# The wide layer norm's sum of squares by two transposes and a VectorE reduction, with two ScalarE steps moved

## The reference

```
x = norm(x + L0(x, adj))   # hypergraph convolution to 512 features, relu, layer norm with gamma and beta,
                           # hypergraph convolution back to 256, + x
x = norm(x + L1(x, adj))   # relu([x, adj @ x / degree] @ W.T)
x = norm(x + L2(x, adj))   # three GCN layers: adj @ (x @ W) + b, relu after the first two
x = norm(x + L3(x, adj))   # relu(adj @ x @ kernel), masked where a row of x is all zero
```

```
var = mean(h * h) - mean(h)**2;  (h - mean) * rsqrt(var + 1e-5) * gamma + beta
```

## Time and profile before

| | |
|---|---|
| time, median of 3 runs | 1382.65 us (1382.41 to 1382.7) |
| the profiled execution's own time | 1382.37 us |
| its span, first to last instruction | 1380.6 us |
| PE busy | 1365.6 us, 99% |
| VectorE (DVE) busy | 1168.3 us, 85% |
| ScalarE (ACT) busy | 1115.1 us, 81% |
| GpSimd (POOL) busy | 1032.8 us, 75% |
| DMA, share of 16 engines, main queue | 16.3% |
| mean granted clock of TensorE | 0.999 |

### The profile page before, as it was taken

How to read it: one execution, slowest core, us unless ns; L and a number is a source line. 1 busy time by engine, 2 the same in 40 slices (tenths; PEclk the granted TensorE clock), 3 DMA queues, 4 the chain that set the end, 5 groups by cost and what they waited for, 6 DMA issues and landing times.

```text
span 1380.6 us, 35393 instructions
## 1 busy us (share of the span) xinstructions
PE 1365.6 (99%) x10836; PEld 1324.6 (96%) x10836; DVE 1168.3 (85%) x4037; ACT 1115.1 (81%) x2584; POOL 1032.8 (75%) x1114
## 2 busy tenths in 40 slices
PE   8999999999999999999999999999999999999997
PEld 7999999999999999999999999999999999999996
DVE  8888888888888888888888888888888888888896
ACT  6777887888888878878878888888788788888776
POOL 5758778778788787787787787877877877878531
PEclk9999999999999999999999999999999999999999
DMA  4101211211211112111112111111121121121000
GB/s 144 36 20 24 47 44 29 47 43 29 44 35 40 44 28 47 44 28 47 43 29 47 36 35 44 28 47 44 29 47 44 29 47 43 28 45 34 2 24 32
DMA packets 45804, 54.45 MB, mean 39 GB/s; under 512 B 12208, under 2 KB 28080, under 8 KB 45616
## 3 DMA queue, kind: packets, MB, share of 16 engines
q1 hardware_dynamic: 45616, 52.19, 16.3%
HBM read 35.33 MB, written 16.83 MB: 38 GB/s over the span
## 4 chain that ended last, share of the span: by engine, by line
PE 97%; ACT 1%; issue 1%; DMA 0%; SPq 0%; DVE 0%; POOL 0%; ACTq 0%; DVEq 0%; POOLq 0%
PE psum L400 95%; PE psum L499 2%; DMA r_f<-w1T_in 0%; PE psum L443 0%; ACT x L1034 0%; SPq L305 0%; ACT tk L1203 0%; ACT h_hi L1015 0%; SPq L338 0%; ACT h_f L1039 0%; DVE n_st L1605 0%; DVE n_s L274 0%; DVE xbw_lo L1670 0%; SPq L342 0%; ACT w1T_hi L1015 0%
## 5 line engine op out<-in xcount | busy, mean ns | idle before, releaser
L1034 ACT ACTIVATE x<-n_s,n_shift,n_rstd 128x256 f32<-128x256 f32 x384 | 208.8, 593 | 4.7 <-DVE n_shift L1629 4.1
L222 POOL TENSOR_TENSOR h_lo<-h_f,h_hi 128x512 fp32r<-128x512 f32 x120 | 155.0, 1292 | 57.7 <-ACT h_hi L1015 56.8
L229 POOL TENSOR_TENSOR r_lo<-r_f,r_hi 128x512 fp32r<-128x512 f32 x123 | 157.3, 1293 | 43.5 <-ACT r_hi L1015 43.5
L2292 POOL TENSOR_TENSOR n_s<-tk,mask 128x512 f32<-128x512 f32 x60 | 62.4, 1041 | 156.2 <-DVE mask L1682 135.2
L1605 DVE BATCH_NORM_STATS2 n_st<-n_s 128x6 f32<-128x256 f32 x384 | 141.9, 412 | 2.2
L400 PE MATMUL psum<-v_hi,h_hi 128*128 128x256 f32 x512 | 137.8, 291 | 2.0 <-ACT h_hi L1015 2.0
L1039 ACT ACTIVATE h_f<-psum,columns 128x256 f32<-128x256 f32 x256 | 107.6, 472 | 35.1 <-PE psum L400 35.0
L400 PE MATMUL psum<-A_f,x 128*128 128x128 f32 x1024 | 135.3, 275 | 0.6 <-ACT x L1034 0.5
L400 PE MATMUL psum<-v_lo,h_hi 128*128 128x256 f32 x512 | 132.7, 281 | 0.0
L400 PE MATMUL psum<-gx_hi,w1T_hi 128*128 128x256 f32 x512 | 132.2, 281 | 0.0
L400 PE MATMUL psum<-gx_hi,w1T_lo 128*128 128x256 f32 x512 | 131.9, 280 | 0.0
(11 more groups left out here) (177 smaller groups left out, 5159.8 us busy)
## 6 DMA issues: line engine op xcount, KB each, us to landing
x_in<-x_in_dram SPq DMA_DIRECT2D x64, 256.0 KB, 2.8
out<-x SPq DMA_DIRECT2D x64, 256.0 KB, 2.0
at_in<-adjT SPq DMA_DIRECT2D x64, 128.0 KB, 2.3
dinv_b<-dinv_row SPq DMA_DIRECT2D x55, 128.0 KB, 4.1
dinv_row<-dinv SPq DMA_DIRECT2D x55, 1.0 KB, 3.1
x<-v_in SPq DMA_DIRECT2D x3, 256.0 KB, 5.8
n_s<-w2T_in SPq DMA_DIRECT2D x2, 256.0 KB, 3.0
r_f<-w1T_in SPq DMA_DIRECT2D x2, 256.0 KB, 5.1
```

Of the source, the lines that this page charges most:

```text
L222: return e.tensor_tensor(dst[1][:], src, f(dst[0][:]), ALU.subtract).then_inc(signal, 1)
L229: e.tensor_tensor(r_s[1][:, half], r_f[:, half], f(r_s[0][:, half]), ALU.subtract).then_inc(r_lo[h], 1)
L1034: last = act.activation(dst[:, g, :], nm.s[:, g, :], ACT.Identity, scale=nm.rstd[:, g:g + 1], bias=nm.shift[:, g:g + 1])
L2292: pool.tensor_tensor(n4.s[:], tk[:], bc(mask[:], [C, 2, D], 2), ALU.mult).then_inc(tk_masked, 1)
```

## The change

The pairs whose squares fall in the loop no longer sum over partitions by matmuls with ones. PE transposes the two halves of `sq1` into columns 384 to 511 of P's two banks, and VectorE reduces these 2 x 128 columns to the two values in column 258, ahead of the variance, in a new step that waits for P's signal and for `h_mean2`. A new semaphore, `sq_added`, stands between it and the variance. In ScalarE's loop `make_x3(n-4)` goes ahead of `root_h(n-1)`, and `copy_h1w(n-3)` ahead of `round_p(n-1)`. Fill and drain keep their order and their matmuls.

```diff
@@ in the semaphores
+        sq_added = sem("sq_added")
@@ PE
             def squares(p):
                 pe.wait_ge(sq_sum, upto(p))
+                if in_loop(p, 1):
+                    for g in range(2):
+                        last = pe.transpose(psum[:, bank("P", p) + g, 3 * C:4 * C], sq1[:, g, :], ident[:])
+                    last.then_inc(pe_did["P"], 1)
+                    return
                 for g in range(2):
                     last = mm(psum[:, bank("P", p) + g, D + 2:D + 3], sq1[:, g, :], ones[:, 0:1], True, True)
                 last.then_inc(pe_did["P"], 1)
@@ ScalarE, body(n)
                 square_mean(n - 1)
                 round_GT(n)
+                make_x3(n - 4)
                 root_h(n - 1)
-                make_x3(n - 4)
+                copy_h1w(n - 3)
                 round_p(n - 1)
-                copy_h1w(n - 3)
                 high_ax3(n - 4)
@@ VectorE
+            def add_columns(p):
+                b = bank("P", p)
+                dve.wait_ge(pe_did["P"], upto(p))
+                dve.wait_ge(hm2, upto(p))
+                if begun(p - 1):
+                    dve.wait_ge(hv, upto(p - 1))
+                dve.tensor_reduce(psum[:, b:b + 2, D + 2], psum[:, b:b + 2, 3 * C:4 * C], AX_X, ALU.add).then_inc(sq_added, 1)
+
             def wide_var(p):
                 b = bank("P", p)
+                if in_loop(p, 1):
+                    add_columns(p)
+                    dve.wait_ge(sq_added, p + 2 - FIRST)
                 h_var = psum[:, b:b + 2, D + 4]
```

## The result

The changed kernel took 1393.31 us (median of 4, 1391.87 to 1393.45) against 1382.56 us for the kernel before, run beside it (4 runs, 1382.41 to 1382.7). The ratio is 1.0071, 95% interval 1.0059 to 1.0083: slower by 0.7%. The forecast was 1393 us.

The account below looks back on a forecast made before the run. PE, busy 99%, was taken to bound the kernel. Cheaper squares give -13.2 us and 55 waits of 0.43 us for x1 add 23.6, so +10.4 on 1382.65 makes 1393.1 us; 8-in-10 range 1384 to 1402.

Parts of the forecast that it names:

- D (p_f): Lateness of p_f on VectorE after the squares' first load, against 1.70: 0.71 us, bounds 0.62 and 0.89.
- p_lo's load, wanted 5.27: PE's load of p_lo: operand ends 5.30 to 5.43, wanted at 5.27; wait of 0.1 to 0.2 us likely.
- xT to squares: PE's work from xT's first load back to the next squares, closing the period's circle: 10.57 us.
- period: One loop iteration, from squares through ScalarE, VectorE, x1 and xT back to squares: 21.22 us against 21.03.
- What PE gains: Squares on PE: two transposes, 0.22 us, replace matmuls of 0.46; 0.24 us an iteration, 13.2 us over 55.
- What the delay costs: x1 0.71 us late makes PE wait 0.43 us at xT in each of 55 iterations: 23.6 us.
- GpSimd's part: GpSimd's scaling of GT ends late, at 0.63, so GT's rounding starts at 0.68 instead of 0.60; adds 0.09.
- rival (a): Only the direct delay counts, GT in time: D 0.62, period 21.13, +5.5 us, 1388 us; chance 0.22.
- The sum: Whole kernel: -13.2 us gained on PE plus 23.6 us of waits, +10.4 us, 1393.1 us; chance 0.46.
- PE's busy share: Sign in the changed profile: PE's busy share falls below 99%.
- Rival (c): Faster: VectorE finds room or the root slips less; PE keeps up to 0.24 us an iteration, 1369.4 us; chance 0.12.
- The rule on transposes: Skill's some 275 ns per transpose on PE: two take 0.55 us, squares cost 0.09 more, 5 us over the loop.

Follow-up runs that it names:

- the version without waits: Changed kernel with GT's rounding behind the root, p_lo ahead of the addition xb on GpSimd, and node_degree ahead of make_p: 1368.06 us, ratio 0.9893.
- The pair of kernels with five equal moves: Gx ahead of Ax3, gx_hi, wide variance, gx_lo and p_lo moved earlier: 1388.75 us with transposes and reduction, 1384.18 us on the kernel before with matmuls.
- the order alone: Kernel before with only ScalarE's new order (x3 ahead of the root, h1w ahead of p's rounding), squares by matmuls: 1394.59 us, ratio 1.0084.
- the short reduction: Changed kernel with VectorE's reduction over 2 instead of 128 columns: 1393.09 us, ratio 1.0068.
- the degrees ahead of p: Changed kernel with VectorE's node_degree (two tiny operations) moved ahead of make_p: 1371.20 us, ratio 0.9912.
- GT's rounding behind the root: Changed kernel with round_GT moved behind root_h on ScalarE: 1385.63 us, ratio 1.0018.
- Gx ahead of Ax3 with transposes: Changed kernel with PE's Gx ahead of Ax3, ScalarE's old order with gx_hi ahead of ax3_hi, wide variance ahead of n4's shift: 1391.40 us, ratio 1.0057.

## Why the prediction was right

Point by point, the forecast beside the row of the kernel after:

| step | forecast | measured |
|---|---|---|
| squares on PE | 0.22 | 0.21 |
| reduction | 0.42 at 0.85 | 0.43 at 0.85 |
| mean's square | 0.53 | 0.52 |
| GT's rounding | 0.68 | 0.68 |
| x3, root | 1.00, 1.98 | 1.00, 1.99 |
| D (p_f) | 0.71 | 0.71 |
| x1 ends | 10.60 | 10.60 |
| p_lo's load, wanted 5.27 | 5.3 to 5.5 | 5.43 |
| xT's first load | 10.65 | 10.66 |
| xT to squares | 10.57 | 10.54 |
| period | 21.22 | 21.20 |

- **What PE gains** was 0.25 us (forecast 0.24), and is shown to be there to take: the version without waits is at 20.75, 0.28 under the old period. Of the other 0.03 the runs show no cause. The pair of kernels with five equal moves does not show the gain, since x1's wait takes more than all of it.
- **What the delay costs** is shown by the order alone (x1's wait without any transpose), by the short reduction (nothing), and by the degrees ahead of p, which takes x1's lateness away while the root stays 0.64 late: 22 us.
- **GpSimd's part** was the least sure term, and the experiment that gives GT 1.3 us sooner confirms it at 5 us against the 4.4 forecast (and rival (a), 1388, is what that kernel did). What was off is a detail: GT ended at 0.58 and not 0.63, and ScalarE followed 0.10 and not 0.05 behind it; the sum was the same.
- **The sum** was 10.4 us, 55 periods of 0.19. The two profiled executions differ by 11.1. Up to the loop's last squares it is 9.2, 0.17 in each of 54 periods. Another 0.56 comes at the start of the drain, at G(62), which in PE's program stands behind n2's shift, late on VectorE by the same path (the trace names no engine for this wait, so the cause is read from the program). The last 1.36 was no part of the forecast: the granted clock fell in the drain of the kernel after. So what was forecast came to 9.7 us, 0.7 under the forecast, and the agreement to 0.2 us between 1393.1 and 1393.31 is luck.
- **One sign failed.** PE's busy share was to fall below 99%; the page says 99% as before (98.5 against 98.9 by its busy times), for the reason given above. And a small slip of the working: 1.00 + 0.99 puts the root at 1.99, as measured, not at 1.98.
- **Rival (c)**, that VectorE has room, was rightly held low for this order, but the room was there: 0.52 us ahead of the root, unused because the next step in the queue could not use it. I weighed it as "VectorE is only at 85%" and did not ask which step could move into the gap.
- **The rule on transposes** in the Trainium skill (TensorE: Matmul & The Clock Gate, Part 4: PE-mode transpose) is not borne out as a cost here: 110 transposes have a mean of 272 ns, near the 275 that the Trainium skill gives, but two of them take 0.21 us between their neighbours' loads. The clock row stays at its top tenth through the loop, with six transposes in each iteration; as they stand among many matmuls, no run shows what transposes alone would earn.

## What to carry to other kernels

When an engine is busy 99% in a fixed cyclic order, taking work from it moves each of its wants forward; so list each operand's margin first (how long it is ready before the engine wants it), and follow the slack of each back round the whole cycle, through queues that seem to have nothing to do with it. A delay on an in-order engine passes one for one to everything behind it unless an idle gap lies between (0.71 us at p_f was 0.71 at x1), so a step moved into the gap that the delay itself makes can cost nothing and give it back: here two tiny operations were worth 22 us. A gap is only room if something in the queue can use it.

## What the runs showed that was not expected

The same wait of 1.72 us near the end left the clock alone in one kernel and not in the other. PE's rows after that wait, kernel after; the eight records of Ax3 take 1.91 us:

```profile
1370.89 0.36 PE L401 MATMUL psum<-v_hi,h_hi 128*128 128x256 f32 x1 [1.72 <-ACT h_hi L1021]
...
1373.09 1.91 PE L401 MATMUL psum<-A_f,x 128*128 128x128 f32 x8
```

The kernel before, same place:

```profile
1361.15 0.36 PE L400 MATMUL psum<-v_hi,h_hi 128*128 128x256 f32 x1 [1.72 <-ACT h_hi L1015]
...
1362.84 1.05 PE L400 MATMUL psum<-A_f,x 128*128 128x128 f32 x8
```

The granted clock over 5 us around the end of the wait (busy of each engine, then the clock) is 0.70 in the kernel after, so the clock lay at its lower level, 1.2 GHz, for part of that stretch, and 1.00 in the kernel before:

```profile
1370.00:1375.00 5.00, 4.11 (x21) 4.01 (x22) 3.12 (x14) 2.44 (x6) 0.00 (x0) 0.70 0.00 0
```
```profile
1360.00:1365.00 5.00, 3.69 (x27) 3.34 (x28) 3.82 (x16) 3.48 (x8) 0.00 (x0) 1.00 0.00 0
```

It cost 1.36 us: from the matmul behind the wait to the end of the span there are 20.81 us in the kernel after and 19.45 before. The wait alone does not decide it. All 14 traces have it. In nine the granted clock over the 5 us from that matmul is 1.00, and 19.4 to 19.5 us follow to the end. In five (the kernel after, the short reduction, GT's rounding behind the root, Gx ahead of Ax3 with transposes, the degrees ahead of p) it is 0.66, and 20.5 to 20.9 us follow. Those five have transposes in the loop, but so have five of the nine. What decides it stays open; a run's time can carry 1.0 to 1.5 us of it that say nothing of the loop. One of the four runs of the changed kernel, 1391.87, is 1.3 to 1.6 us under the others, which would fit a run without it; no trace of that run shows it.
